# A four-layer graph network on one core: row gathers of the edge passes held to two groups ahead of TensorE

## The reference

```python
# L1, attention with 8 heads of 16 columns
k_j = k[src] + e
v_j = v[src] + e                       # e = edge_attr @ We
logits = jnp.sum(q[dst] * k_j, axis=-1) / np.sqrt(C)
m = jax.ops.segment_max(logits, dst, num_segments=n)
ex = jnp.exp(logits - m[dst])
denom = jax.ops.segment_sum(ex, dst, num_segments=n)
agg = jax.ops.segment_sum(alpha[..., None] * v_j, dst, num_segments=n)   # alpha = ex / denom[dst]
# L2, twice: 3 heads of 128 columns, then 1 head of 128
e = leaky_relu(el[src] + er[dst], 0.2)
alpha = exp(e - segment_max(e)[dst]) / segment_sum(...)[dst]
out = jax.ops.segment_sum(alpha[:, :, None] * feat[src], dst, num_segments=n) + h @ res_w.T + bias
```

## Time and profile before

| what | value |
|---|---|
| median of 3 runs | 3552.42 us (3545.26 to 3560.50) |
| span of the profiled execution | 3550.1 us |
| PE busy | 2464.1 us (69%) |
| DVE busy | 1418.4 us (40%) |
| POOL busy | 1354.0 us (38%) |
| ACT busy | 962.5 us (27%) |
| mean granted TensorE clock | 0.743 of full |
| `attn` pass, first gather to last evacuation | 661.0 to 1415.7 us |
| `gat1` pass | 1571.7 to 2270.5 us |
| `gat2` pass | 2445.2 to 3100.3 us |

### The profile page before, as it was taken

The page is one execution under the profiler, slowest core; times in us unless marked ns, Lnnn a source line. Parts: engine busy times, 40 slices in busy tenths (PEclk is TensorE's granted clock), DMA queues, the critical chain, the costliest instruction groups (busy, mean ns, idle before and its releaser), DMA issues.

```text
span 3550.1 us, 36582 instructions
## 1 busy us (share of the span) xinstructions
PE 2464.1 (69%) x12427; PEld 1828.4 (52%) x12427; DVE 1418.4 (40%) x3070; ACT 962.5 (27%) x2050; POOL 1354.0 (38%) x1417
## 2 busy tenths in 40 slices
PE   4999997377666766545677666664565655649998
PEld 3666665256555555333444444443564555526666
DVE  6756555244444455533333333431221212251423
ACT  3422223122222222442333333231221222220202
POOL 3000002645444553375555555045565555320000
PEclk9777788677777787667888888776555555569999
DMA  9388641456666674124555655322344444346362
GB/s 210 115 300 297 234 147 39 139 167 189 175 177 180 177 199 142 26 55 125 169 184 172 189 181 186 107 70 52 88 112 95 106 105 103 94 137 205 116 205 66
DMA packets 518595, 517.78 MB, mean 146 GB/s; under 512 B 154128, under 2 KB 463763, under 8 KB 517227
## 3 DMA queue, kind: packets, MB, share of 16 engines
q1 hardware_dynamic: 310349, 267.24, 24.9%
q0 software_dynamic: 50528, 115.22, 13.3%
q10 hardware_dynamic: 157534, 132.98, 11.9%
HBM read 301.13 MB, written 227.33 MB: 149 GB/s over the span
## 4 chain that ended last, share of the span: by engine, by line
PE 40%; another core or an unknown queue 25%; DVE 12%; issue 12%; ACT 6%; DMA 2%; POOL 1%; ACTq 0%; DVEq 0%; SPq 0%
PE ps L1613 9%; PE ps L1540 8%; PE ps L1434 6%; PE ps L1444 5%; ACT arena L1052 4%; DVE arena L2224 2%; DMA ends_gat<-arena 1%; PE ps L1522 1%; DVE arena L2286 1%; PE ps L1589 1%; PE ps L1573 1%; PE ps L1584 1%; DVE arena L1934 1%; DVE arena L2227 1%
## 5 line engine op out<-in xcount | busy, mean ns | idle before, releaser
L1052 ACT ACTIVATE arena<-ps 128x544 f32<-128x544 f32 (+9 forms) x591 | 485.9, 825 | 1746.1 <-remote 874.5
L1613 PE MATMUL ps<-arena 128*128 128x136 f32 (+2 forms) x2352 | 695.9, 460 | 376.3 <-ACT arena L1052 194.6
L1021 POOL DMA_INDIRECT arena<-t_gat,src_i x784 | 741.9, 946 | 537.1 <-DVE arena L2286 307.8
L1613 PEld LDWEIGHTS ps<-arena 128*128 128x128 f32 x2352 | 479.6, 269 | 516.4 <-issue 425.2
L1021 POOL DMA_INDIRECT arena<-t_attn,src_i x392 | 375.4, 958 | 344.1 <-DVE arena L2286 225.3
L2257 DVE TENSOR_TENSOR_SCAN arena<-arena,ps 64x128 f32<-64x128 f32 (+2 forms) x147 | 60.0, 408 | 803.0 <-remote 714.2
L1540 PE MATMUL ps<-arena 128*128 128x384 bf16 x1850 | 308.2, 331 | 37.6 <-issue 25.1
L1589 PEld LDWEIGHTS ps<-arena 128*128 128x128 f32 x1568 | 288.3, 268 | 45.2 <-issue 22.5
L1589 PE MATMUL ps<-arena 128*128 128x3 f32 (+1 forms) x1568 | 266.6, 292 | 15.7 <-issue 15.7
L1540 PEld LDWEIGHTS ps<-arena 128*128 128x128 bf16 x1850 | 183.1, 99 | 162.4 <-issue 46.0
L2286 DVE TENSOR_TENSOR arena<-arena,ps 128x1536 f32<-128x1536 f32 (+1 forms) x196 | 230.6, 1218 | 38.7 <-ACT arena L1189 30.1
(11 more groups left out here) (320 smaller groups left out, 2942.1 us busy)
## 6 DMA issues: line engine op xcount, KB each, us to landing
ends_gat<-arena ACTq DMA_DIRECT2D x98, 774.0 KB
arena<-adj_hbm SPq DMA_DIRECT2D x90, 640.0 KB, 4.2
same_b<-same_hbm SPq DMA_DIRECT2D x294, 128.0 KB
adj_hbm<-arena SPq DMA_DIRECT2D x9, 3200.0 KB, 11.8
ends_attn<-arena ACTq DMA_DIRECT2D x98, 272.0 KB
ends_gat<-arena ACTq DMA_DIRECT2D x98, 258.0 KB
arena<-edst SPq DMA_DIRECT2D x98, 256.0 KB, 4.2
starts_q<-zrow SPq DMA_DIRECT2D x28, 896.0 KB, 6.8
```

Of the source, the lines that this page charges most:

```text
L1021: g.indirect_dma_start(out=row_b[:, n % RB, k, 0:row_tab[p].shape[1]], out_offset=None, in_=row_tab[p], in_offset=bass.IndirectOffsetOnAxi ...
L1052: return a.activation(o, i, ACT.Copy)
L1613: i = mm(o, same_f[:, g % RB, k, :], msg[:, g % 4, k * W:(k + 1) * W], start=True, stop=True)
```

## The change

A constant `AHEAD` = 2, and in POOL's loop over the groups one wait more: before the four gathers of group n, from n = 2 on, POOL waits until PE has done the destination rows of group n-2. The older waits stay. All three passes have the loop, so 288 waits are added and nothing else is touched.

```diff
+AHEAD = 2
...
                 for n in range(NG):
+                    if n >= AHEAD:
+                        pool.wait_ge(dst_done.sem, dst_done.at(p, n, AHEAD))
                     if n >= RB:
                         pool.wait_ge(rows_in.of(n), rows_in.at(p, n, 1))
                         pool.wait_ge(msg_done.sem, msg_done.at(p, n, RB))
```

## The result

The kernel before takes 3550.35 us (median of 4 runs, 3545.26 to 3560.50), the changed one 3275.22 us (4 runs, 3258.09 to 3285.66): a ratio of 0.9221 with a 95% interval of 0.9183 to 0.9258. The forecast was 3422 us. Its sign and its range (3150 to 3620) held, its size did not: -130 us forecast, -275 measured.

A forecast was written before the change was run, and what follows sets the result against it. The prediction took the edge passes to be bound by waits for PE's counts, late while POOL issues gathers. Heads -82 and running pitch -48 made -130 us: 3550.1 to 3420, or 3422 beside the median; range 3150 to 3620.

The forecast's parts named there:

- What bounds the kernel: Edge passes: bound by waiting, as PE's counts arrive late while POOL issues gathers, clearing some 3 us after it stops.
- The wait itself, and two groups of lead: POOL's gathers: met waits cost nothing visible; rows needed 12.4 us after release have some 7 us to spare, cost nothing.
- The running pitch: All three passes: bursts of eight, 6.9, 6.4 and 6.4 us a group; -35, -26 and +13, sum -48 us.
- short bursts don't stall, the pitch halfway: All passes: bursts of four may end before the stall; halfway pitch 5.7, 3190 us; chance 0.18 for 2986 to 3190.
- The heads: Pass starts: eight gathers at once, not 32, so DVE follows PE's records; -23.6, -27.9, -30.5, sum -82 us.
- The evacuation near 698: Sign of being right, after the head of `attn`: first evacuation near 698 us instead of 721.
- that rival: DMA engines: loads queued behind gathers hold the engines up; worth at most 28.7 us, 3524; within stall unchanged, chance 0.18.
- Lockstep: Passes: four gathers hold PE's next count until 3.05 us after them; pitch 7.75, up to 3767 us, chance 0.22.

The follow-up runs named there:

- e6_plain: Kernel before with POOL's indirect gathers replaced by plain DMAs of 128 consecutive rows, same bytes: 2804.04 us, 0.7952 of the kernel before.
- e9_from8_again: Kernel before plus the new wait only from group 8 of each pass on, on a chip with late counts: 3270.15 us, 0.9272 of the kernel before.
- e13_pairs: Kernel before plus the new wait before even groups only, two groups back: 3272.20 us, 0.9307 of the kernel before.
- e11_quads: Kernel before plus a wait before every fourth group only, for the destination rows four back: 3600.54 us, 1.0241 of the kernel before.
- e1_first8: Kernel before plus the new wait for groups 2 to 7 of each pass only, on the chip without late counts: 2963.18 us, 1.0055.

## Why the prediction was right in sign and short in size

**What bounds the kernel: right.** The prediction read the "remote" waits as counts of PE that come late while POOL issues gathers. `e6_plain` takes the indirect issuing away and has no such wait in the passes. Over all waits of the kernel before for PE's sums and turned logits and maxima, sorted by where in a burst the product ended: of those that ended within 2.5 us of a burst's start 10 of 90 were seen over 0.5 us late, at 2.5 to 7.5 us about half (88 of 178), and of those that ended more than 7.5 us into it all but two (134 of 136), by 12 us (median) at 7.5 to 10 us. So in a burst of sixteen, 19.7 us, some two thirds are lost to everyone who waits for PE; in one of eight the last quarter and a part of the middle.

**The wait itself, and two groups of lead: right.** In the gat passes DVE's terms waited 26.2 us in 13 pieces for rows, in `attn` not at all. Where the new wait is met it costs nothing that shows: from the last gather of a group to the first of the next within a burst it is 0.305 us (median), as before.

**The running pitch: the step that failed.** -48 us forecast, -237 measured. The form of the step held: bursts of eight and a pause behind, released within 0.2 us of the late counts, without the 3.3 us of the messages. Its size was wrong in two numbers, both taken from the wrong rows.

- The stall behind a burst was put at 3.05 us, read behind a burst of sixteen. It depends on the length. In the changed kernel the late counts clear (median) 1.75 us after a burst of eight, 1.1 after one of four and 2.4 to 2.5 after one of twelve. The kernel before had it to be read: some 1.8 us behind its own eights and 2.9 to 3.1 behind its sixteens. With it the step reads (9.7 + 1.75)/2 = 5.7 us, and the passes came to 5.89, 5.97 and 5.70.
- The pitch of 6.9 taken for `attn` was six groups' mean over a stretch with bursts of eight that messages released. The row between them in the earlier trace rows gave the period of the bursts themselves, 11.40 us from 1274.82 to 1286.22, with a pause of 1.69: 5.7 us a group. There DVE's two messages (1284.79 to 1286.07) happened to be done as soon as a late count would have cleared. It is what a cycle comes to without the wait for late messages, and it was quoted and passed over.

The rival "short bursts don't stall, the pitch halfway", 5.7 us and 3190, had the right pitch by a wrong reason: the bursts of eight do stall, but shortly. Added to the heads as they came out, 41 us, pitches of 5.7 throughout make 97 x (1.45 + 0.92 + 0.52) + 41 = 321 us; `attn` and `gat1` came out some 0.2 to 0.3 us above it.

**The heads: half of it, and most of that given back.** The step said that DVE would follow PE's records, and so it does, up to the first terms and scans. In `attn`, the first terms and POOL's release, then the scan behind the first held burst, and the first evacuation (this answers the earlier trace rows):

```profile
671.77 1.22 DVE L2227 TENSOR_TENSOR arena<-arena,ps 128x1024 f32<-128x1024 f32 x1 [29.12 <-PE ps L1587]
671.95 0.94 POOL L1024 DMA_INDIRECT arena<-t_attn,src_i  x1 [7.91 <-PE ps L1587]
...
683.43 0.41 DVE L2260 TENSOR_TENSOR_SCAN arena<-arena,ps 64x128 f32<-64x128 f32 x1 [5.91 <-remote]
683.63 0.94 POOL L1024 DMA_INDIRECT arena<-t_attn,src_i  x1 [1.98 <-remote]
...
697.66 0.94 POOL L1024 DMA_INDIRECT arena<-t_attn,src_i  x1 [0.30 <-issue]
700.79 0.62 ACT L1055 ACTIVATE arena<-ps 128x544 f32<-128x544 f32 x1 [11.91 <-remote]
```

The evacuation near 698 was forecast, from a start at 661.0, and it came at 700.79 from a start at 654.3, which is 9.5 us worse. A second burst, twelve gathers from 683.63 to 698.60, held the count of the first sums. In `gat1` and `gat2` it is plainer (this answers the earlier trace rows):

```profile
1443.49 0.94 POOL L1024 DMA_INDIRECT arena<-t_gat,src_i  x1 [6.26 <-PE ps L1592]
...
1446.90 0.41 DVE L2260 TENSOR_TENSOR_SCAN arena<-arena,ps 24x128 f32<-24x128 f32 x1 [1.51 <-PE ps L1600]
...
1467.21 0.94 POOL L1024 DMA_INDIRECT arena<-t_gat,src_i  x1 [0.30 <-issue]
...
1472.07 1.46 ACT L1055 ACTIVATE arena<-ps 128x1548 f32<-128x1548 f32 x1 [20.27 <-remote]
...
2256.83 0.60 ACT L1055 ACTIVATE arena<-ps 128x516 f32<-128x516 f32 x1 [13.52 <-remote]
```

The scan comes 19.4 us after the first gather, 17.1 forecast, and then PE's next counts pass in time too, each lets POOL have another group, and twenty gathers go out in one burst. The first evacuation waits 20.27 us, until 3.9 us after its end. The step had taken the head up to the first group's terms and left out the burst that comes next.

What remained is paid back once the running part has the wait too. Whoever issues 32 gathers first has eight groups in store. In the trace of `e9_from8_again`, which has the old heads, the first evacuations come 59.3, 55.1 and 47.2 us after the first gathers, 36 us later than in the changed kernel, but its pitches are 5.75, 5.87 and 5.59, and from first gather to last evacuation its three passes take 1830.5 us against 1828.0. The prediction said that the lost lead "is in the pitch", and priced it at nothing there.

**A reading of rows 1.** "The waits that end with a load are 28.7 us in all" left out a row that is not in the earlier trace rows: PE waited 22.0 us, once, for the edge attributes at the head of `attn`. The bound of that rival is 51 us and not 29, and it changes nothing in the verdict on it.

**Lockstep: did not happen.** It needed four gathers to hold the next count for 3.05 us. Behind fours the delay was 1.1 us, and more than four fifths of the groups went out in bursts of eight and more (all but 51 of 294).

**The clock.** The prediction left TensorE's clock out. Granted in the pass windows (us, PE busy, PEld, DVE, ACT, POOL, granted clock, DMA share, GB/s), before and after, `attn` and `gat2`:

```profile
721.00:1415.00 694.00, 487.56 (x2732) 408.33 (x2732) 341.97 (x522) 178.24 (x424) 344.84 (x360) 0.75 0.63 177
...
2497.00:3100.00 603.00, 350.82 (x1619) 339.99 (x1619) 130.66 (x424) 128.97 (x381) 338.75 (x359) 0.50 0.43 101
```

```profile
701.00:1272.00 571.00, 448.82 (x2711) 384.64 (x2712) 340.97 (x517) 174.50 (x425) 349.94 (x364) 0.83 0.75 215
...
2257.00:2810.00 553.00, 353.04 (x1613) 340.26 (x1614) 129.66 (x424) 127.60 (x381) 345.26 (x367) 0.50 0.47 111
```

In `attn` the clock rises from 0.75 to 0.83 of 2.4 GHz, between its two levels, and PE's busy time falls by 39 us; in `gat2` it is 0.50, the 1.2 GHz level, in both. So `gat2` gained 0.52 us a group with no help of the clock. How much of the 1.26 us of `attn` is the clock's no run parts. The 59 us that PE no longer loses before its edge terms lie in the same pass, and their share isn't parted either.

## What to carry to other kernels

Where an engine's issuing holds back the counts of another, look at how long it issues without a pause before you look at how much it issues: the same 392 gathers a pass cost 250 us less in bursts of eight (`e13_pairs`) than in the kernel before with its sixteens, and 328 less than in `e11_quads`. Hold the producer by a count of the stage that suffers, of fine grain, and not by the place in the ring alone; and read a stall from bursts of the length that the change will make. Time it on more than one chip: where the trouble is absent, so is the gain.

## What the runs showed of the hardware that was not expected

- **Chips differ by a fifth on the same program.** The kernel before takes 3550, 3527 and 3524 us on three sets of runs, two of them known to be on different chips, and 2945 us on another chip. No trace of the kernel before was taken there, but `e1_first8`, which is that kernel from group 8 on, has no "remote" wait and POOL issues 384 gathers back to back. Why the one chip has no late counts isn't known; data and POOL times (0.95 us a gather, 0.30 between) are the same on both.
- **Indirect DMAs issued by POOL delay counts of PE**, also when they bring 32 bytes a partition. Plain DMAs issued by POOL, of full rows, don't: 0.7952 of the time.
- **The delay grows over the first 7.5 us of a burst** (before: late are 42 of 86 at 2.5 to 5 us, 46 of 92 at 5 to 7.5, 66 of 68 at 7.5 to 10) and clears some 1.1, 1.8, 2.4 and 3 us after a burst of four, eight, twelve and sixteen. In the changed kernel more counts look late early in a burst (108 of 220 in the first 5 us against 52 of 176), but not all are PE's: 24 of the 108 are evacuations that waited for a store. With the "remote" waits alone it is 54 of 220 against 28 of 176.
- **In the longest bursts PE itself falls behind.** The 59.2 us of idle time before its edge terms in `attn` (68.7 in `e11_quads`, 0.2 with the change, none in `e13_pairs` and `e6_plain`) end with no releaser. So what is held up is more than the visibility of a count; what it is, and whether it would be there in an execution that leaves no records of its instructions, no run shows.
